# First attention of a two-layer transformer kernel: pairs of probability tiles added by DMA, eight GpSimd additions, one block of sums on TensorE

## The reference

```python
q = _qdq(x) @ _qdq(wq).T + bq
kv = cond @ wkv.T + bkv
k, v = jnp.split(kv, 2, axis=-1)
attn = jax.nn.softmax(jnp.einsum('bnhd,bmhd->bhnm', q, k) * scale, axis=-1)
o = jnp.einsum('bhnm,bmhd->bnhd', attn, v).reshape(B, N, C)
out = _qdq(o) @ _qdq(wp).T + bp
```

## Time and profile before

| | |
|---|---|
| median of three runs | 2556.49 us (2553.41 to 2556.79) |
| the profiled execution | 2554.09 us |
| its span | 2552.3 us |
| TensorE, share of the span | 98% |
| VectorE / ScalarE / GpSimd | 70% / 48% / 48% |
| first attention, from about 629 to 1372 us | 743 us |
| mean granted TensorE clock | 0.997 of full speed |

### The profile page before, as it was taken

The page is one execution under the profiler, slowest core; times in us unless marked ns, Lnnn a source line. Parts: engine busy times, 40 slices in busy tenths (PEclk is TensorE's granted clock), DMA queues, the critical chain, the costliest instruction groups (busy, mean ns, idle before and its releaser), DMA issues. The chain is left out here.

```text
span 2552.3 us, 34124 instructions
## 1 busy us (share of the span) xinstructions
PE 2509.1 (98%) x13393; PEld 1630.9 (64%) x13408; DVE 1789.8 (70%) x2456; ACT 1215.9 (48%) x1853; POOL 1218.2 (48%) x325
## 2 busy tenths in 40 slices
PE   8999999999999999999999999999999999999998
PEld 8988898987555555555545787788533333335786
DVE  4554554546777777777765667664899999999873
ACT  4222212311665665666663232322688888886110
POOL 0000000000998989989882000000599999997410
PEclk9999999999999999999999999999999999999999
DMA  8677786655636345353414754443997777776300
GB/s 305 204 264 234 260 291 241 218 162 167 129 72 127 74 99 107 69 122 83 98 42 169 240 170 170 144 157 98 248 212 166 168 162 166 160 171 197 114 33 34
DMA packets 218865, 405.11 MB, mean 159 GB/s; under 512 B 18216, under 2 KB 94536, under 8 KB 218640
## 3 DMA queue, kind: packets, MB, share of 16 engines
q1 hardware_dynamic: 218704, 402.93, 57.1%
HBM read 260.63 MB, written 140.59 MB: 157 GB/s over the span
## 5 line engine op out<-in xcount | busy, mean ns | idle before, releaser
L1414 ACT ACTIVATE probs<-psum 128x512 f32<-128x512 f32 (+1 forms) x832 | 438.6, 600 | 316.1 <-PE psum L1241 313.7
L1439 DVE TENSOR_REDUCE win_max<-psum 128x1 f32<-128x802 f32 x480 | 455.0, 987 | 138.6 <-PE psum L1206 134.4
L2349 DVE TENSOR_SCALAR probs<-psum,bound 128x1024 f32<-128x1024 f32 (+1 forms) x416 | 499.0, 1275 | 30.5 <-POOL pooled L2381 22.9
L2324 ACT ACTIVATE probs<-probs 128x1024 f32<-128x1024 f32 (+1 forms) x416 | 437.4, 1058 | 81.8 <-DVE probs L2349 40.1
L2381 POOL TENSOR_TENSOR pooled<-pooled,probs 128x2048 f32<-128x2048 f32 x92 | 424.0, 4609 | 13.1 <-POOL pooled L2381 0.4
L1551 POOL TENSOR_TENSOR pooled<-pooled,probs 128x2048 f32<-128x2048 f32 x93 | 426.3, 4584 | 7.3
L312 POOL TENSOR_TENSOR r_q<-ve_q,minus_half 128x4 f32<-128x4 f32 x8 | 8.7, 1084 | 611.6 <-DVE ve_q L256 611.6
L1241 PE MATMUL psum<-q_st,k_st 128*128 128x512 f32 (+1 forms) x832 | 295.3, 422 | 4.7 <-ACT probs L1414 2.8
L1206 PE MATMUL psum<-k_st,q_st 96*128 96x402 f32 x960 | 274.1, 366 | 2.7 <-DVE win_max L1439 2.2
L1206 PEld LDWEIGHTS psum<-k_st,q_st 96*128 96x128 f32 x960 | 165.9, 189 | 153.7 <-DVE win_max L1439 126.3
L2292 PE MATMUL psum<-q_st,k_st 128*128 128x512 f32 (+1 forms) x832 | 253.2, 430 | 9.3 <-DVE probs L2349 8.2
(11 more groups left out here) (277 smaller groups left out, 4304.0 us busy)
## 6 DMA issues: line engine op xcount, KB each, us to landing
k_st<-k_hi SPq DMA_DIRECT2D x64, 801.0 KB, 10.3
k_st<-k_lo SPq DMA_DIRECT2D x48, 801.0 KB, 11.0
k_hi<-kt_hi SPq DMA_DIRECT2D x32, 801.0 KB
k_lo<-kt_lo SPq DMA_DIRECT2D x32, 801.0 KB
v_rows<-v_out SPq DMA_DIRECT2D x96, 256.0 KB
v_st<-v_rows SPq DMA_DIRECT2D x24, 768.0 KB
q_st<-q_hi SPq DMA_DIRECT2D x64, 256.0 KB, 8.1
w<-w_hi_d SPq DMA_DIRECT2D x64, 256.0 KB, 3.1
```

The costliest lines, as they stand in the source:

```text
L1414: A.activation(probs[i % NPROBS][0:rows, j, :], bank(score_banks.where["score", u, t, j])[0:rows, :], ACT.Exp, scale=1.0 / ROOT).then_inc( ...
L1439: V.tensor_reduce(win_max[:, r, j, c:c + 1], window(windows.where["max", u, i])[:, :, 0:MV], AX.XY, ALU.max).then_inc(max_done, 1)
L2324: A.activation(dst, dst, ACT.Exp, scale=1.0 / ROOT).then_inc(exp_done, 1)
L2349: V.tensor_scalar(probs[i % NPROBS][0:rows, half * W:half * W + W, :], window(("score", u, t, half))[0:rows], bound[0:rows, u // NG, t:t + 1],
```

## The change

In units 0 to 14, GpSimd issues three DMAs per unit that add one tile onto another in SBUF (`accum_op=ALU.add`): tile 1 onto 0, 5 onto 4 and 9 onto 8. GpSimd then adds tiles 2, 3, (0+1), 6, 7, (4+5), 10, 11 and (8+9) with eight additions. TensorE sums only tile 12 and `pooled`, both in step 5. Steps 3 and 4 become ordinary steps. The six DMAs of `load_kq` wait for scores of steps 1, 2, 4, 5, 7 and 8, and `load_v` stands behind them on SyncE's queue. In the last two units `closing` moves from step 6 to step 7. `first_codes` keeps its step but comes behind its last score.

```diff
-            SUM_AT, CODES_AT, ROWS_AT = 4, 3, 7
-            NADD, POOLED_LAST = 9, 7
-            POOLED = NADD + 1
+            SUM_AT, CODES_AT, ROWS_AT = 5, 3, 7
+            PAIRS, NADD, POOLED_LAST = ((0, 1), (4, 5), (8, 9)), 8, 7
...
-                    return u == 0 or not (t in (SUM_AT - 1, SUM_AT) and (t, j) > (SUM_AT - 1, 1) or t == SUM_AT + 1 and j == 0)
+                    return u == 0 or not (t == SUM_AT and j > 0 or t == SUM_AT + 1 and j == 0)
...
+                def pair_landed(u, p):
+                    d = len(PAIRS) * u + p
+                    return pair_added[d % 2], 16 * (d // 2 + 1)
...
-                    if u < UNITS - 1 and t >= POOLED:
-                        return lone_read, (TT - POOLED) * u + t - POOLED + 1
-                    return pool_added, added(u, max(t, 1) if t else 3)
+                    if u == UNITS - 1:
+                        return pool_added, added(u, max(t, 1) if t else 3)
+                    if t == TT - 1:
+                        return lone_read, u + 1
+                    for p, (first, second) in enumerate(PAIRS):
+                        if t == second:
+                            return pair_landed(u, p)
+                    return pool_added, added(u, {0: 2, 2: 3, 3: 1, 4: 5, 6: 3, 7: 4, 8: 8, 10: 6, 11: 7}[t])
...
+                    def sums(u):
+
+                        if u == 0:
+                            M.wait_ge(set_up, 1)
+                        take_den(u)
+                        lone_sum(u, TT - 1, start=True).then_inc(lone_read, 1)
+                        pooled_sum(u)
...
                         elif t == SUM_AT:
                             maxima(0)
+                            if u:
+                                sums(u - 1)
+                            maxima(1)
                             scores(u, t, 1)
-                            if u:
-                                lone_sums(u - 1, [TT - 1])
-                                pooled_sum(u - 1)
-                            maxima(1)
                             scores(u, t, 2)
                             maxima(2)
                             values_behind()
                             scores(u, t, 3)
-                        elif t == SUM_AT - 1:
-                            scores(u, t, 1)
-                            values_behind()
-                            if u:
-                                lone_sums(u - 1, [POOLED])
-                            maxima(0)
-                            scores(u, t, 2)
-                            maxima(1)
-                            scores(u, t, 3)
-                            if u:
-                                lone_sums(u - 1, [POOLED + 1])
-                            maxima(2)
-                            if now == (UNITS - 1, CODES_AT):
-                                first_codes()
...
+                    def add_pair(u, p):
+
+                        d, (first, second) = len(PAIRS) * u + p, PAIRS[p]
+                        G.wait_ge(exp_done, score(u, second, HPG))
+                        G.wait_ge(tile_read, tile(u, first) + 1)
+                        if d >= 2:
+                            G.wait_ge(pair_added[d % 2], 16 * (d // 2))
+                        G.dma_start(flat(of(u, first)), flat(of(u, second)),
+                                    accum_op=ALU.add).then_inc(pair_added[d % 2], 16)
...
+                    add_pair(0, 0)
+                    for u in range(UNITS - 1):
+                        start = of(u, 2)
+                        G.wait_ge(tile_read, tile(u, 2) + 1)
+                        add(u, 1, start, start, 3, exps_of(u, 3))
+                        add(u, 2, start, start, PAIRS[0][0], pair_landed(u, 0))
+                        add_pair(u, 1)
                         if u:
                             G.wait_ge(summed, u)
-                        add(u, 3, pooled, start, 3, exps_of(u, 3))
-                        for k in range(4, POOLED if u < UNITS - 1 else POOLED_LAST):
-                            add(u, k, pooled, pooled, k, exps_of(u, k))
+                        add(u, 3, pooled, start, 6, exps_of(u, 6))
+                        add(u, 4, pooled, pooled, 7, exps_of(u, 7))
+                        add(u, 5, pooled, pooled, PAIRS[1][0], pair_landed(u, 1))
+                        add_pair(u, 2)
+                        add(u, 6, pooled, pooled, 10, exps_of(u, 10))
+                        add(u, 7, pooled, pooled, 11, exps_of(u, 11))
+                        add(u, 8, pooled, pooled, PAIRS[2][0], pair_landed(u, 2))
+                        if u + 1 < UNITS - 1:
+                            add_pair(u + 1, 0)
...
                         for quarter in range(NQ):
                             rows = slice(quarter * DH, (quarter + 1) * DH)
+                            Y.wait_ge(scored, score(u - 2, 1 + 3 * quarter, 0))
                             load(k_st[s][rows, :, :], (k_hi, k_lo, k_hi)[quarter][0][u].rearrange("(j d) t -> d j t", d=DH),
                                  kq_landed[s])
+                            Y.wait_ge(scored, score(u - 2, 2 + 3 * quarter, 0))
                             load(q_st[s][rows, :, :], (q_hi, q_hi, q_lo)[quarter][0][u].rearrange("(j d) t -> d j t", d=DH),
                                  kq_landed[s])
...
                         if u + 2 < UNITS:
-                            if u + 2 >= NSLOT:
-                                Y.wait_ge(scored, score(u, 0, 0))
                             load_kq(u + 2)
```

More of the change, by code:

```diff
@@ L1126, in attention_0 @@
                 tile_read, lone_read, pool_added, summed = sem("tile_read"), sem("lone_read"), sem("pool_added"), sem("summed")
+                pair_added = [sem(f"pair_added{i}") for i in range(2)]
                 acc_copied, den_copied = sem("acc_copied"), sem("den_copied")
@@ L1398, in pe_program @@
                             scores(u, t, 3)
+                            if now == (UNITS - 1, CODES_AT):
+                                first_codes()
                             if now == (UNITS - 1, ROWS_AT):
@@ L1544, in of, with flat @@
                         return probs[tile(u, t) % NPROBS]
+                    def flat(buffer):
+                        return buffer[:].rearrange("p j q -> p (j q)")
+                    def add_pair(u, p):
[6 more added lines that the diff above has]
+                                    accum_op=ALU.add).then_inc(pair_added[d % 2], 16)
                     def add(u, k, out, before, tile_of, ready):
@@ L1554, in exps_of @@
                         return exp_done, score(u, t, HPG)
[L1556 to L1560, removed]
+                    add_pair(0, 0)
[5 more added lines that the diff above has]
+                        add_pair(u, 1)
                         if u:
                             G.wait_ge(summed, u)
-                        add(u, 3, pooled, start, 3, exps_of(u, 3))
-                        for k in range(4, POOLED if u < UNITS - 1 else POOLED_LAST):
-                            add(u, k, pooled, pooled, k, exps_of(u, k))
+                        add(u, 3, pooled, start, 6, exps_of(u, 6))
[7 more added lines that the diff above has]
+                            add_pair(u + 1, 0)
+                    u = UNITS - 1
+                    start = of(u, 0)
+                    G.wait_ge(tile_read, tile(u, 0) + 1)
+                    add(u, 1, start, start, 1, exps_of(u, 1))
+                    add(u, 2, start, start, 2, exps_of(u, 2))
+                    G.wait_ge(summed, u)
+                    add(u, 3, pooled, start, 3, exps_of(u, 3))
+                    for k in range(4, POOLED_LAST):
+                        add(u, k, pooled, pooled, k, exps_of(u, k))
                     root_on_pool(nm, 0)
```

## The result

The changed kernel takes 2541.96 us, median of 5 runs (2535.15 to 2544.16), against 2554.29 (2553.19 to 2556.79) for 5 runs of the kernel before; the medians differ by 12.3 us. The ratio is 0.9943 with a 95% interval of 0.9932 to 0.9954, which is 14.6 us less (11.7 to 17.4). The kernel is faster, clear of noise, by less than half of the forecast gain of 32.5. The forecast was 2524. The time lies in the stated range of 2517 to 2550, but on the ground of the third rival (GpSimd binds a little), which had a chance of 12%.

A forecast was written before the change was run, and what follows sets the result against it. TensorE's written order, with its loop with VectorE, was taken as the bound, GpSimd a close second. Gains of 30.2 + 0.8 + 1.5 = 32.5 us left 2521.6 profiled, hence a median of 2524, range 2517 to 2550.

The forecast's parts named there:

- the third rival: GpSimd binds a little: issues and stalls of 6.5 to 8.6 us a unit give back part; halfway 2538; chance 12%.
- TensorE's part: First attention: two blocks of sums fewer take 2.16 us off each of units 1 to 14, 30.2 us.
- the 1.71 us of the old step 4: Excess of old step 4's two blocks of sums over ordinary steps; the new step 5 should cost the same.
- The pairs: Adding DMAs: 9.3 us hidden behind two additions; (0,1) has longer; (4,5) stalls GpSimd 2.9 us in company of loads.
- the 3.2 that I had left: GpSimd's spare us in a unit of 43.74, after eight additions of 37.26 and three issues of 3.3.
- my signs of being wrong: Additions 5 or 8 waiting over 3 us together, GpSimd over 95% in a unit, or ScalarE waiting in step 4.
- The issue: Issuing a pair's DMA from GpSimd: 1.1 us each, ends 0.5 and 4.0; three a unit are 3.3.
- the second rival: The issue is dear: at 4.0 us each the unit is 49.3 us, the whole 2601; chance 3%.
- The landing: A pair's transfer within SBUF: 8.3 us, between 6.5 and 11.5; (4,5) up to 12.2 in company of loads.
- Buffers: Tile 8 comes free 3.6 us into the next unit, step 4 begins at about 5.1; other tiles have more room.
- The loads: Spread over steps 1 to 8, needed 16.7 us after the last issue, only 1 MB before it: nothing.
- The odd units: Gains of 0.8 us in unit 0 and 1.5 in unit 15; unit 14 counted at 2.16 like units 1 to 13.

The follow-up runs named there:

- the run without pairs: All three adding DMAs of each unit and the waits for them left out of the changed kernel: 2525.06 us, ratio 0.9885.
- the run with the loads between the pairs: Changed kernel with the six loads of keys and queries waiting for scores of steps 0, 0, 1, 1, 9 and 10: 2530.31 us, ratio 0.9902.
- the halved pairs: Changed kernel with each pair's DMA adding only the columns of heads 0 and 1, same issues and waits: 2525.21 us, ratio 0.9885.
- the burst: Changed kernel with the loads of keys and queries back in one burst at a unit's first score: 2589.65 us, ratio 1.0138.

## Why the prediction was right or wrong

**TensorE's part: right, a little too large.** The excess of step 3 went, but the new step 5 costs more than the 1.71 us of the old step 4. Window 2 of step 4 to values of step 6 is 7.63 us (911.69 to 919.32) against 5.70, so 1.93. That the exchanged order costs the same was wrong by 0.2; my lower end, two blocks at 1.96, is what the run without pairs gives (1.97). For 13 units that is 2.5 us of the 9.5 by which their forecast missed. The other 7 are the pairs'.

**The pairs: the failed step.** "Each pair is used two additions after its issue, so 9.3 us are hidden" holds for (4,5) and (8,9). "The first pair's addition waits for the previous unit's last and for the values of tile 2, and has longer" is wrong. Only one addition of 4.6 us lies between, and the wait for tile 2 is nothing but the spare time itself. In the sum, pair (0,1) should have been charged with its landing less the issue of 1.1 us (which the sum has already) and one addition of 4.66: with my own 8.3 that is 2.5 us. Pair (4,5), reckoned alike with my own 12.2 in company, has 1.1 and 9.3 to cover it and costs 1.8. Together they are 4.3 against the 3.2 that I had left. I had held (4,5)'s wait against the 3.2 as if no other stood in the chain. Written down so, the unit is 44.9 us, and the likeliest case would have been the third rival, and not the forecast. Measured, from 814 to 1174 us (8.1 units), GpSimd waited 31.0 us for pairs before addition 2 and 8.1 before addition 5, 4.8 us a unit, in the view of waits (us in total, times, longest):

```profile
POOL probs L1559 <- DMA probs<-probs: 31.0, 8, 4.6
...
ACT probs L1409 <- POOL pooled L1559: 20.1, 12, 2.7
...
POOL pooled L1559 <- DMA probs<-probs: 8.1, 7, 1.9
```

The unit of 44.55 us is about 37.3 for additions, 1.9 for issues, 4.8 for these waits and what is left, 0.5. Issues and stalls are 6.7 us, at the lower end of the 6.5 to 8.6 that the third rival gave. Of my signs of being wrong, ScalarE did wait for GpSimd in step 4; the wait of more than 3 us stood before addition 2, where I had not looked, and additions 5 and 8 together waited 1.0 a unit.

**The granted clock: a term that the sum lacks.** The prediction prices waits at their own length. In unit 14 a wait of 2.65 us was followed by 6.8 us with the clock at 0.50, which cost 3.2 more: together 5.9 of the 6.3 us by which unit 14 exceeds that of the run with the loads between the pairs (50.85 against 44.52). In unit 0 it was 2.96 us of wait and 3.4 at low clock.

**The issue.** I took 1.1 us. The row shows 0.87 to 0.90, of which the next addition waits 0.6; the halved pairs say that it costs nothing. It is a little less than I took, and the second rival falls.

**The landing.** Undisturbed, 6.9 to 7.3 us for a tile in the kernels with other places for the loads, between my lower end of 6.5 and the 8.3 I took. The target that is read as well does not double it. In company of loads (4,5) took 9.9 to 11.9, near the 12.2 forecast. The Trainium skill (DMA: Bandwidth & Descriptors, Queues, rings and completion order) has the DMA engines take turns between queues. The trace agrees that a pair isn't held until the loads are through, but taking turns from the issue on is not what it shows. Half a pair issued with a load of keys of 1.6 times its bytes landed 2.7 us behind it (10.0 against 7.3): its queue moved nothing for 4.9 us and then had 71% of the engines' time against 33% for the loads. In the burst, pair (8,9) of unit 8 moved nothing for 7.1 us and landed 8.2 after that. What holds the queue in these first microseconds is open.

**Buffers.** That addition 8 would end before ScalarE needs tile 8's buffer (3.6 us into the unit against 5.1) was computed without stalls; with them it is the link by which the lateness reaches TensorE. Tile 4's, needed in step 0 of the next unit, I had passed over in "The other tiles have a step or more".

**The loads.** "Spread, only 1 MB stands before it: nothing" was asked for the wrong party. They landed in time for TensorE, as forecast; what they cost, they cost the pairs.

**The odd units.** Unit 0 (+3.1 instead of -0.8) and unit 14 (+4.4 instead of -2.2) were costed on TensorE alone. I named what SyncE moves in the ordinary unit and left out what it moves there: two values' loads, 1.6 MB of copies and a load of keys and one of queries ahead of the first pair, which took 18.1 us, and 3.1 MB beside the last one of unit 13. These two units are 10.5 of the 19.4 us by which the forecast missed the profiled execution, the low clock included; units 1 to 13 are 9.5, and unit 15 gave 0.5 more than forecast.

## What to carry to other kernels

A transfer put between two steps of an engine has to be charged with its landing less the work that really stands between issue and use. Spare time counts once for the whole chain, and not for each wait in it. A stall can cost more than its own length: here TensorE's clock stood at half for 3.4 to 13.7 us during and behind the longer ones, so look at the granted clock behind a stall before its price is set. When a queue of transfers becomes part of a chain, look at every other transfer in its company, the odd first and last units included: here moving six loads by a few steps was worth 12 us, and undoing their spreading cost 48, part of it through the clock, though the same spreading without the pairs was worth nothing.

## What the runs showed of the hardware that I had not expected

An adding DMA from SBUF to SBUF of 128 x 2048 float32 landed in 6.9 to 7.3 us with the engines to itself, half of it in 4.5 to 4.9. By an estimate from these two sizes that is about 5 us for a megabyte, the rate of the plain loads (211 GB/s, rows 10), and some 2 us fixed; a plain copy of the same tile wasn't run beside it. A half pair in company of a load took 10.0 to 10.7 us, more than twice its time alone, and most of the difference passed before its first packet (4.9 us after the issue instead of 1.4; 7.1 in a burst of 3.2 MB). A pair's issue lasts 0.87 us on GpSimd; the next addition starts 0.6 us after it began and lasts 4.87 instead of 4.58. TensorE's granted clock went to 0.50 during or just behind each of the eleven waits of 2.3 to 6.2 us that the traces of these runs have in the first attention, for 3.4 to 13.7 us, and a block of sums then took 1.93 us instead of 1.07.
